# Second and fourth layer of a four-layer model: heads on TensorE's two row halves, projections in three fp32r parts, stacks in DRAM with rows outermost

## The reference

```
h   = concat([c, x], axis=1)                          # 512 keys for each batch
q   = (x @ q_w + q_b)  as 16 heads of 16
kv  = (h @ kv_w + kv_b) as 16 heads of 16, k and v interleaved in the last axis
a   = softmax(where(mask, q . k / 16, -inf))
y   = (a . v) @ out_w + out_b + x
y   = rmsnorm(y) * postnorm_w
out = gelu(y @ mlp_w1 + mlp_b1) @ mlp_w2 + mlp_b2 + x
```

## Time and profile before

| | before |
|---|---|
| median of 3 runs (lowest to highest) | 1430.48 us (1427.15 to 1430.51) |
| the profiled execution's own time | 1426.24 us |
| its span, first to last instruction | 1424.5 us |
| mean granted PE clock | 0.949 of 2.4 GHz |
| busy: PE, DVE, ACT, POOL | 89%, 73%, 50%, 36% |
| second layer, turn and projections | 743.6 to 789.1 us |
| second layer, attention | 789.1 to 918.4 us |
| fourth layer, turn and projections | 1174.0 to 1220.7 us |
| fourth layer, attention | 1220.7 to 1349.2 us |

### The profile page before, as it was taken

How to read it: one execution, slowest core, us unless ns; L and a number is a source line. 1 busy time by engine, 2 the same in 40 slices (tenths; PEclk the granted TensorE clock), 3 DMA queues, 4 the chain that set the end, 5 groups by cost and what they waited for, 6 DMA issues and landing times. The chain is left out here.

```text
span 1424.5 us, 27768 instructions
## 1 busy us (share of the span) xinstructions
PE 1269.5 (89%) x9018; PEld 1026.3 (72%) x9018; DVE 1033.9 (73%) x2398; ACT 709.3 (50%) x1502; POOL 513.8 (36%) x667
## 2 busy tenths in 40 slices
PE   4799999999699999998699799869599949799969
PEld 4699999998599999997585466558377735456558
DVE  5788887787688888887646688574488866688574
ACT  3466665566566566666412265441266612156541
POOL 2654454552554554440303000030299913000030
PEclk8899999999899999999899799989799989799989
DMA  4201100000211100000206333120640015444110
GB/s 147 61 15 31 31 29 29 29 22 4 97 31 31 31 29 22 29 15 0 93 1 199 75 79 84 27 76 18 205 97 3 2 49 181 84 86 85 30 63 31
DMA packets 74157, 80.14 MB, mean 56 GB/s; under 512 B 7940, under 2 KB 59895, under 8 KB 73547
## 3 DMA queue, kind: packets, MB, share of 16 engines
q1 hardware_dynamic: 73612, 78.86, 20.3%
q10 hardware_dynamic: 446, 0.05, 0.0%
HBM read 61.08 MB, written 17.57 MB: 55 GB/s over the span
## 5 line engine op out<-in xcount | busy, mean ns | idle before, releaser
L1859 DVE TENSOR_REDUCE s_mx<-s_s_ps 128x1 f32<-128x512 f32 x256 | 173.2, 689 | 47.8 <-PE s_s_ps L1930 42.4
L1835 ACT ACTIVATE s_probT<-s_st_ps 128x1024 f32<-128x1024 f32 x128 | 129.1, 1025 | 131.5 <-PE s_st_ps L1951 131.4
L777 ACT ACTIVATE a_prob<-a_s_ps,a_negmax 128x257 f32<-128x257 f32 x256 | 119.2, 476 | 96.3 <-DVE a_negmax L867 96.2
L720 POOL TENSOR_TENSOR x_v_hi<-a_v_sum,x_one 128x512 fp32r<-128x512 f32 x60 | 63.2, 1054 | 253.8 <-DVE a_v_sum L856 253.7
L1930 PE MATMUL s_s_ps<-l_k_st,l_q_st 127*128 127x512 f32 x256 | 126.9, 507 | 16.4 <-PEq L1323 12.7
L1609 POOL TENSOR_SCALAR s_below<-s_masked,s_mx 128x256 f32<-128x256 f32 x256 | 118.6, 485 | 28.6 <-DVE s_mx L1637 28.5
L882 DVE TENSOR_TENSOR a_pT_lo<-a_t_ps,a_pT_hi 128x512 fp32r<-128x512 f32 x128 | 88.2, 689 | 36.5 <-ACT a_pT_hi L790 34.6
L1930 PEld LDWEIGHTS s_s_ps<-l_k_st,l_q_st 127*128 127x128 f32 x256 | 51.9, 204 | 77.6 <-DVE s_mx L1859 41.6
L1815 POOL COPY l_v_st<-l_v_all 128x256 f32<-128x256 f32 (+1 forms) x32 | 12.6, 404 | 257.2 <-PE s_o_ps L1962 197.5
L867 DVE TENSOR_REDUCE a_negmax<-a_s_ps 128x2 f32<-128x514 f32 x128 | 86.7, 687 | 21.4 <-PE a_s_ps L924 20.1
L1637 DVE CUSTOM_DVE_ANT_0 s_masked<-s_s_ps,l_mask 128x256 f32<-128x256 f32 x256 | 90.7, 420 | 15.7 <-PE s_s_ps L1674 15.7
(11 more groups left out here) (248 smaller groups left out, 3980.6 us busy)
## 6 DMA issues: line engine op xcount, KB each, us to landing
l_k_st<-k_stack SPq DMA_DIRECT2D x96, 128.0 KB
l_q_st<-q_stack SPq DMA_DIRECT2D x96, 64.0 KB, 2.2
x_wqk_raw<-L_xattn_wq SPq DMA_DIRECT2D x32, 128.0 KB, 2.2
x_wqk_raw<-L_xattn_wk SPq DMA_DIRECT2D x32, 128.0 KB, 2.2
x_wv_raw<-L_xattn_wv SPq DMA_DIRECT2D x16, 256.0 KB, 3.0
a_wo_raw<-L_xattn_wo SPq DMA_DIRECT2D x16, 256.0 KB, 3.1
k_stack<-p_k_hi SPq DMA_DIRECT2D x4, 1024.0 KB, 5.2
k_stack<-p_k_lo SPq DMA_DIRECT2D x4, 1024.0 KB, 6.1
```

Of the source, the lines that this page charges most:

```text
L777: nc.scalar.activation(prob[:, n % 2, qt, 0:NK], s_ps[:, n % 2, qt, 0:NK], ACT.Exp, bias=negmax[:, n % 2, qt:qt + 1], accum_out=den[:, n % ...
L1835: nc.scalar.activation(probT[:, (s + 2) % U, n], st_ps[:, 2 * (n % 2):2 * (n % 2) + 2].rearrange("p k t -> p (k t)"), ACT.Exp).then_inc(z. ...
L1859: nc.vector.tensor_reduce(mx[:, s, n:n + 1], s_ps[:, n % 2, 0:c.NK], AX.X, ALU.max).then_inc(z.max_done, 1)
```

## The change

For the second and fourth layer `small_projections` and `small_attention` become `pair_projections` and `pair_attention`.

- Two heads stand in the two row halves of one tile: rows 0 to 49 and rows 64 to 113. Row 48 of a half meets the mask and row 49 the maximum; the zero rows and their memsets go. S is now four steps of two matmuls (one in each half, 512 columns each, into two banks), and DVE takes the maxima of both heads, 1024 columns, in one instruction. E is eight steps of two matmuls of 256 columns, with three one-bank buffers in place of two of two banks, and ACT takes exponentials of 512 columns.
- The projections split x and the weights and use three fp32r matmuls; the turning of x is in the same block. ACT and DVE read the product from PSUM. The weights of the next layer are loaded and split in the MLP of the first layer and in `project_out` of the third. v is written straight into the layout that P reads, and POOL's copy for each quad goes.
- The DRAM stacks have the channel outermost, then batch and token. The first 64 channels (near) are stored first, then the next 64 (far); when the near ones have landed SP loads units 0 and 1 (a unit is two batches of four heads, 12 transfers), then stores the second 128 channels. The block ends when everything has landed.
- In the attention SP issues units 2 and 3, 24 transfers, in iteration 0. From iteration 4 on it issues half a unit, six transfers, behind the row of maxima. The row goes out as two transfers. The quads run over the batches first. The result of P and the turned maxima share a PSUM bank, so P0 also waits for the maxima of its own iteration to be read out.

```
+def load_unit(c, sp, q_stack, k_stack, q_st, k_st, v, sem, halves=range(2)):
+    HD, (g, part) = c.HD, divmod(v, 2)
+    bs, slot = slice(2 * part, 2 * part + 2), g % 2
+    k_heads, q_heads = [stack.rearrange("u (h d) b n -> u h d b n", d=HD) for stack in (k_stack, q_stack)]
+    for half in halves:
+        heads = slice(4 * g + half, 4 * g + 4, 2)
+        for n in range(3):
+            rows = slice(half * c.HALF + n * HD, half * c.HALF + (n + 1) * HD)
+            sp.dma_start(k_st[rows, slot, :, bs].bitcast(F32).rearrange("r a b n -> r a (b n)"),
+                         k_heads[(0, 0, 1)[n], heads, :, bs].rearrange("a d b n -> d a (b n)")).then_inc(sem, 16)
+            sp.dma_start(q_st[rows, slot, :, bs].bitcast(F32).rearrange("r a b t -> r a (b t)"),
+                         q_heads[(1, 0, 0)[n], heads, :, bs].rearrange("a d b t -> d a (b t)")).then_inc(sem, 16)
...
+                near, far, whole = slice(0, P // 2), slice(P // 2, P), slice(0, P)
+                for is_k, count in ((True, first_k), (False, first_q)):
+                    for part in range(2):
+                        sp.wait_ge((z.qk_hi, z.qk_lo)[part], count)
+                        store(sp, is_k, part, 0, near, z.stored_first)
+                for is_k in (True, False):
+                    for part in range(2):
+                        store(sp, is_k, part, 0, far, z.stored)
+                sp.wait_ge(z.stored_first, 4 * 16)
+                loaded = load_unit(c, sp, q_stack, k_stack, q_st, k_st, 0, z.first_in)
+                load_unit(c, sp, q_stack, k_stack, q_st, k_st, 1, z.second_in)
+                for is_k, count in ((True, first_q + first_k), (False, 2 * first_q)):
+                    for part in range(2):
+                        sp.wait_ge((z.qk_hi, z.qk_lo)[part], count)
+                        store(sp, is_k, part, 1, whole, z.stored)
...
+    pe_steps = steps("S0 E0 E1 S1 M0 E2 E3 P0 P1 E4 E5 S2 P2 P3 S3 E6 E7 X0")
+    act_steps = steps("E0 E1 E2 E3 E4 E5 O0 E6 E7")
+    dve_steps = steps("S0 M0 S1 S2 S3 X0")
...
+                    if first == 0:
+                        load(2, range(2))
+                        load(3, range(2))
+                    if second is not None:
+                        g, b = batch(second)
+                        sp.wait_ge(z.mx_out, second + 1)
+                        for half in range(2):
+                            m = half * HALF + c.MAX_ROW
+                            sp.dma_start(q_st[m:m + 1, g % 2, :, b].bitcast(F32),
+                                         mxT[2 * half:2 * half + 2, second % 2].bitcast(F32)
+                                         ).then_inc(row_in[second % 2], 16)
+                    if first is not None and first >= 4 and first // 2 + 2 < units:
+                        load(first // 2 + 2, (first % 2,))
...
+                def scores(n, i):
...
+                    wait(pe, z.max_done, NS * i + n - 1)
+                    a, qt = n // QT, n % QT
+                    for half in range(2):
+                        q, k = tiles(half, c.MAX_ROW, i)
+                        mm = nc.tensor.matmul(s_ps[:, n % 2, half], q[:, a, qt * P:(qt + 1) * P], k[:, a],
+                                              start=True, stop=True)
...
+                def shifted(n, i):
...
+                        pe.wait_ge(row_in[i % 2], 32 * (i // 2 + 1))
+                    u = NE * i + n
+                    wait(pe, z.exp_done, u - 2)
+                    a, pair, half = n // 4, n // 2 % 2, n % 2
+                    q, k = tiles(half, c.MAX_ROW + 1, i)
...
+                    if kt == 0:
+                        pe.wait_ge(z.exp_done, NE * (i + 1))
+                        wait(pe, z.x_out, i)
+                        pe.wait_ge(z.mx_out, min(i + 3, c.quads))
```

More of the change, by code:

```diff
@@ new lines, in _ @@
+                for n, (src, b) in enumerate(tiles):
+                    wait(pe, z.v_out, n - 3)
+                    parts = ((core.c_hi, core.c_lo), (x_hi, x_lo))[src]
+                    for j in range(QT):
+                        tok = slice((QT * b + j) * P, (QT * b + j + 1) * P)
+                        for kt in range(KT):
+                            mm = product(turned[:, n % 4, j * D:(j + 1) * D], [x[:, kt, tok] for x in parts],
+                                         (core.wkv_hi[:, 1, kt], core.wkv_lo[:, 1, kt]), kt == 0, kt == KT - 1)
+                    mm.then_inc(z.v_done, 1)
@@ new lines, in _, with turned_high, high @@
+            @block.scalar
+            def _(act):
+                def turned_high(n):
+                    kt, cols = chunks[n]
+                    act.wait_ge(z.tile_turned, n + 1)
+                    nc.scalar.activation(x_hi[:, kt, cols], turned[:, n], ACT.Copy).then_inc(z.x_hi_done, 1)
+                def high(g):
+                    act.wait_ge(z.qk_done, g + 1)
+                    nc.scalar.activation(places(q_hi, k_hi, g), qk_ps[:, g % 4].rearrange("p (b t) -> p b t", t=S),
+                                         ACT.Identity, bias=bias(g)).then_inc(z.qk_hi, 1)
+                for n in range(len(chunks)):
+                    turned_high(n)
+                for g in range(len(groups)):
+                    high(g)
@@ new lines, in pair_attention, with rounds, quad, batch @@
+    HD, NKT, HALF, NQ = c.HD, c.NKT, c.HALF, c.NQ
+    NS, NE = 4, 8
+    units = c.quads // 2
+    pe_steps = steps("S0 E0 E1 S1 M0 E2 E3 P0 P1 E4 E5 S2 P2 P3 S3 E6 E7 X0")
+    act_steps = steps("E0 E1 E2 E3 E4 E5 O0 E6 E7")
+    dve_steps = steps("S0 M0 S1 S2 S3 X0")
+    def rounds(body):
+        def quad(i):
+            return i if 0 <= i < c.quads else None
+        for i in range(c.quads + 3):
+            body(quad(i), quad(i - 1), quad(i - 2), quad(i - 3))
+    def batch(q):
+        return q // B, q % B
@@ L1992, in project_out @@
[L1992 to L2000 removed]
+        s_ps, st_ps = st.psum("s_ps", [P, 2, 2, 512]), st.psum("st_ps", [P, 3, 512])
@@ L2007, in _, with load, body @@
             def _(sp):
+                def load(v, halves):
+                    wait(sp, z.st_done, NE * 2 * (v - 3))
+                    load_unit(c, sp, q_stack, k_stack, q_st, k_st, v, unit_in[v % 4], halves)
+                def body(first, second, third, fourth):
+                    if first == 0:
[11 more added lines that the diff above has]
+                        load(first // 2 + 2, (first % 2,))
@@ new lines, in _, with body @@
+                rounds(body)
+            @block.scalar
+            def _(act):
+                def body(first, second, third, fourth):
+                    for kind, n in act_steps:
+                        if kind == "E" and third is not None:
+                            u = NE * third + n
+                            act.wait_ge(z.st_done, u + 1)
+                            wait(act, z.o_done, third - 1)
+                            nc.scalar.activation(probT[:, third % 2, n // 4, n // 2 % 2, n % 2], st_ps[:, u % 3],
+                                                 ACT.Exp, scale=c.scale).then_inc(z.exp_done, 1)
+                        elif kind == "O" and fourth is not None:
+                            act.wait_ge(z.o_done, fourth + 1)
+                            wait(act, z.x_done, fourth)
+                            nc.scalar.activation(oT[:], o_ps, ACT.Copy).then_inc(z.o_out, 1)
+                rounds(body)
@@ new lines, in project_out, with _ @@
+def project_out(core, name, c, o_all, wo, bo, dst, next_layer=None):
+    nc, ins = core.nc, core.ins
+    with core.stage(name) as st:
+        w_sb, b_row, oT = st.sb("w", [P, KT, D]), st.sb("b_row", [P, D]), st.sb("oT", [P, KT, T])
+        t_ps, y_ps = st.psum("t_ps", [P, 4, 512]), st.psum("y_ps", [P, 4, 512])
+        w_in, b_in, turned, t_out, x_ready, y_done, y_out = [
+            st.sem(n) for n in ("w_in", "b_in", "turned", "t_out", "x_ready", "y_done", "y_out")]
+        next_in, next_hi = st.sem("next_in"), st.sem("next_hi")
+        per = P // c.W
+        with nc.Block() as block:
+            @block.gpsimd
+            def _(pool):
+                core.clear_used(pool)
+                if next_layer:
+                    core.split_low(pool, next_hi)
+            @block.scalar
+            def _(act):
+                if next_layer:
+                    core.split_high(act, next_in, next_hi)
+            @block.sync
+            def _(sp):
```

648 lines of the change are left out of this document (234 added, 414 removed).

## The result

The changed kernel takes 1436.57 us (median of 6 runs, 1434.51 to 1440.71) beside 1429.76 us of the kernel before on the same chip: a ratio of 1.0049, with a 95% interval of 1.003 to 1.0068. The forecast was 1421.5 us and faster. The time lies in the stated range of 1391 to 1441 us, but the direction is wrong: the change made the kernel slower, beyond the interval.

A forecast was written before the change was run, and what follows sets the result against it. PE's order of steps was taken to bound the attention. Two layers of -7 us attention and +2 us projections, plus 1 us, give -9 us: 1417 against the profiled 1426.2, 1421.5 beside the median of 1430.5; range 1391 to 1441.

The forecast's parts named there:

- emptying: End of the attention, iterations 16 to 18: eight exponentials set the pace, 13.4 us against 17.2, a gain of 3.8.
- turn and projections: Projection block: PE work falls to 30 us, but transfers end the block at 47.5 us against 45.5, 2 us lost per layer.
- filling: Start of the attention, up to E0 of quad 0: loses 3.2 us per layer, 1 us of it from iteration 2 at 1.2 GHz.
- iterations 2 to 15: Steady part of the attention: 6.6 us per iteration instead of 7.06, between 6.4 and 7.3, 6.4 us less for each layer.
- the rest: Splitting the next weights, in the third layer's `project_out`: costs 1 us, up to 4.5 us if wholly behind that block's work.
- the landing of the first row: Attention's filling: first row of maxima leaves at 9.8 us behind 2.36 MB, lands at 13 to 19 us, taken as 15.5.
- E0: First E step of a quad on PE; in the filling, quad 0's was to wait for the row's transfer, 13.3 us before.
- E3: Last of the four E steps on PE in an iteration of the kernel before; the four were put at 1.9 us.
- the ring: Steady iteration: S3, its maximum, X0, S0, M0, then P0 waits for DVE's read-out; next S3 starts at 6.6 us.
- the third: Rival, chance 0.22: block 52 us, first row at 19 us, 1437 us; decides once block and filling lose over 10.2 us per layer.
- The second rival: Transfers hide: block 39 us, row landed by 13 us, iterations of 6.4 us, attention 116 us, 1392 us in all; chance 0.22.
- the fourth: Rival: row halves bring nothing, by issue order or draining at shape changes; iterations of 7.3 us, 1441 us; chance 0.10.

The follow-up runs named there:

- first experiment: Changed kernel with the 24 transfers of units 2 and 3 issued behind the rows of maxima of quads 0, 1 and 2: 1417.67 us, ratio 0.9918.
- the earlier turning: Changed kernel with PE turning the maxima one step earlier and DVE reading them out before its S0: 1418.81 us, ratio 0.9928.

## Why the prediction was wrong

Against the forecast of -9 us the spans give +8.7. The 17.7 us between them, term by term. To size the iterations and the emptying as the prediction did, the first E of iteration 16 is needed. It stands at 902.59 and 1342.61 us in the changed kernel and at 903.12 and 1333.88 in the kernel before:

```profile
902.17 0.50 PE L1930 MATMUL s_s_ps<-l_k_st,l_q_st 127*128 127x512 f32 x1
902.51 0.64 PE L1951 MATMUL s_st_ps<-l_q_st,l_k_st 128*128 128x256 f32 x4
902.99 0.38 PE L1980 MATMUL s_x_ps<-ident,s_oT 128*128 128x128 f32 x2
903.12 0.72 PE L1951 MATMUL s_st_ps<-l_q_st,l_k_st 128*128 128x256 f32 x4
```

| us, second and fourth layer | forecast | measured | off, together |
|---|---|---|---|
| turn and projections | +2, +2 | +2.6, +4.0 | 2.6 |
| filling | +2.2, +2.2 | +5.8, +8.2 | 9.6 |
| iterations 2 to 15, with 1 us at half clock | -5.4, -5.4 | -8.6, -4.7 | -2.6 |
| emptying | -3.8, -3.8 | +0.1, -0.6 | 7.1 |
| the rest | +1 | +2.0 | 1.0 |

- **The step that failed is the landing of the first row, 9.6 us of the 17.7.** The prediction said that the row "lands at 13 to 19 us; I take 15.5". It took 19.1 and 21.5. The mechanism was right (E0 waits for the row, the row for the 24 loads); the size was not. The 2.36 MB were bounded by 140 and 217 GB/s, and they ran at 126 and 110, below both. The 217 had been worked out from 78 GB/s at a share of 0.36 as if rate and share went together; here a share of 0.89 and 0.93 gave 126 and 110. The 140 came from a burst of 2 us. SP's issuing was too low as well: 9.8 us for 24 loads, where the prediction's own row (three in 1.38) gives 11.0, and 13.2 and 11.4 were measured. It is not what set the landing, though: in the fourth layer SP was faster and the row was later. The first experiment shows the cause: without those loads ahead of it the row is in place after 10.2 us.
- **The emptying gained almost nothing, 7.1 us of the 17.7.** The prediction let iteration 15 of the kernel before end at 901.2. The lines above show its last scores and its E3 behind that point, and the next E at 903.12. So 1.9 of the 17.2 us belonged to the iterations, which took 7.19 us each and not 7.06, and the emptying took 15.3. In the changed kernel it takes 15.4 and 14.7 instead of 13.4: from X of iteration 15 to the last X the steps are 5.7, 5.0 and 3.5 us (902.23, 907.90, 912.93, 916.47), and the 1.5 us from there to the end of the block had no term.
- **The iterations gained more in the second layer, -3.2 us, and less in the fourth, +0.7.** The steady iteration was right: 6.48 us against 6.6, with the ring as its cause, shown by the earlier turning. That its gain came out larger is the other side of the edge at 901.2. The half clock lasted for two iterations, not one: from the second read-out to the fourth 14.8 us passed instead of 13.0. In the fourth layer two later iterations took 8.0 us instead of 6.5.
- **The projections, 2.6 us.** The second layer's 48.1 us is nearly the forecast 47.5. PE through after 31 us, stores out of 64 partitions in 15 us, and a wait at the end all came as written. The fourth layer's block starts at half clock (granted clock 0.58 from 1175.3 to 1179.0): the turn takes 3.34 us instead of 1.94, and the first store leaves 9.6 us after PE's first turn instead of 8.2. The other 1.3 us of the difference between the layers were not traced.
- **The rest, 1.0 us.** The forecast put it into the third layer's `project_out`, and there nothing shows: from its first matmul to the next block's first 26.2 us passed before and 26.1 after. The time lies between the second layer's `project_out` and the third layer's projections (77.0 us before, 79.9 after, of which 0.8 come back later); its cause is open.

Of the rivals, the third (the transfers in half the partitions are the bound twice) came true in kind: the first row at 19 us was its number, the block at 52 was not. That its time of 1437 us is the measured one is partly luck. It set 26 us of loss against 20 of gain, and 20.6 and 13.9 were measured; block and filling together lost 8.4 and 12.2 us, but against gains of 8.5 and 5.4 and not of the 10.2 that its threshold supposed. Of the signs that the prediction had named, the ring, the row halves and the wait for the row came as written (only the transfers behind PE's last matmul ran at 255 GB/s, where under 250 was named); they tell its mechanism and say nothing of its sizes. The second rival (transfers hide) is excluded by the 16.9 us of wait, the fourth by 6.48 us. Nothing in the iterations asks for a drain of PE at a change between half rows and full rows: an S pair costs 0.32 us ahead of P and 0.34 ahead of E.

## What to carry to other kernels

A short transfer that an engine waits for has to be issued ahead of the bulk loads on the same queue; count all the bytes that stand in front of it at a rate measured on transfers of the same shape, and do not scale a rate by the busy share of the DMA engines. Before pricing a phase of a pipeline, look in the timeline for the instruction that starts it: a window's edge that is 2 us off moved 2 us from one term to another here. When a long stage is sped up, look for the ring of waits, and test the named releaser by moving one step: it can name an engine that was done long ago. And when compute falls below the transfers of a block, the next gain is in which transfers the block really has to wait for.

## What was not expected of the hardware

- The rate went with the shape of the transfers, at DMA shares of 0.83 to 1.04: 336 GB/s from 128 partitions, 203 from 64, 131 and 153 into 16, and 184 when two queues carried such loads. With two rows as the outermost dimension it was 65 GB/s at a share of 0.19.
- The issuing engine itself is held by its queue: each of the last two far stores took SP over 2.2 us to issue, where a load took 0.42.
- PE's clock fell to 1.2 GHz for some microseconds in a steady stretch of the changed kernel (1283.0 to 1291.5: granted clock 0.80, PE busy 7.7 of 8.5 us, and 16 matmuls of P took 1.77 us in place of 1.07), twice in the fourth layer and not in the second. The kernel with the rows ahead shows such iterations of 8.0 us in its second layer too, the one with iterations of 6.0 us none. The clock stayed there for 73 us in the kernel with both matmuls in one half, busy 98% of the time. What lifts it again was not found.

```profile
1283.00:1291.50 8.50, 7.73 (x64) 4.04 (x64) 5.91 (x9) 4.86 (x11) 0.00 (x0) 0.80 0.60 90
```
